# An iterated layer-norm stage: where the constant is added, how two of eight tiles are centred, and how the bias products are shaped

## The reference, cut to what matters

```
def _L1_ffn_ref(x, ln_w, ln_b, W, b):        # C = 128, EPS = 1e-5, 30 iterations
    def step(h, _):
        h = h + 0.01 * jnp.tanh(h)
        h = h * jax.nn.sigmoid(h)
        h = _layernorm(h, ln_w, ln_b)
        h = jnp.einsum('bsc,dc->bsd', h, W) + b
        return (h, None)
    x, _ = jax.lax.scan(step, x, None, length=N_ITERS)
    return x
...
x = x + _L1_ffn_ref(_layernorm(x, axis=-1), ...)
```

## Time and profile before

| | us |
|---|---|
| median of 3 runs | 1390.7 (1389.99 to 1391.48) |
| the profiled execution | 1390.53 |
| its span, first to last instruction | 1388.6 |
| TensorE's share of the chain of waits that ended last | 78% |
| granted TensorE clock, mean over the span | 0.985 of full speed |
| the iterated stage in it, from about 616 to 1364 | 748 |

### The profile page before, as it was taken

One profiled execution on the slowest core, in us unless ns is written; L12 is line 12 of the kernel. 1 busy time (PEld: TensorE's weight loads), 2 busy tenths in 40 slices (PEclk: granted clock), 3 DMA queues, 4 the chain that ended last, 5 costly groups with the idle time before them and its releaser, 6 DMA issues.

```text
span 1388.6 us, 28231 instructions
## 1 busy us (share of the span) xinstructions
PE 1332.4 (96%) x8786; PEld 1085.0 (78%) x8786; DVE 1234.2 (89%) x2774; ACT 1011.1 (73%) x1373; POOL 948.3 (68%) x749
## 2 busy tenths in 40 slices
PE   4899999999999999869999999999999999999998
PEld 3677777777777776558888888888888888888887
DVE  6678888887788886599999999999999999999997
ACT  1344444444444444569999999999999999999994
POOL 2244444444444444269999999999999999999995
PEclk9899999999999999969999999999999999999999
DMA  5111111111111100000000000000000000000004
GB/s 178 39 39 38 38 38 38 38 38 38 38 38 38 37 0 1 0 1 0 0 0 0 0 0 0 0 0 0 0 0 0 0 0 0 0 0 0 0 0 122
DMA packets 29790, 27.68 MB, mean 20 GB/s; under 512 B 3269, under 2 KB 21448, under 8 KB 29640
## 3 DMA queue, kind: packets, MB, share of 16 engines
q1 hardware_dynamic: 29768, 27.41, 6.2%
HBM read 23.21 MB, written 4.19 MB: 20 GB/s over the span
## 4 chain that ended last, share of the span: by engine, by line
PE 78%; DVE 11%; issue 4%; ACT 3%; POOL 1%; SPq 1%; DMA 0%; DVEq 0%; ACTq 0%; POOLq 0%
PE psum L751 34%; PE psum L763 15%; PE psum L747 6%; PE psum L553 4%; PE psum L555 4%; PE psum L554 4%; PE psum L694 3%; PE psum L570 2%; PE psum L575 2%; ACT emb_f L855 2%; PE psum L584 2%; DVE emb_n L1177 1%; DVE x_less_n L1161 1%; PE psum L564 1%; DVE xh L1059 1%
## 5 line engine op out<-in xcount | busy, mean ns | idle before, releaser
L751 PE MATMUL psum<-w_t,y_all 128*128 128x128 f32 x3840 | 493.7, 282 | 0.0
L751 PEld LDWEIGHTS psum<-w_t,y_all 128*128 128x128 f32 x3840 | 447.9, 192 | 54.5 <-issue 54.5
L454 POOL TENSOR_TENSOR f_rs<-f_var,half_neg 128x8 f32<-128x8 f32 x240 | 410.4, 1710 | 49.2 <-DVE f_var L1116 30.2
L1091 DVE BATCH_NORM_STATS2 f_stat<-g_ring 128x6 f32<-128x256 f32 x960 | 340.7, 413 | 3.9 <-ACT g_ring L813 3.9
L458 POOL TENSOR_TENSOR h_ring<-g_ring,f_rs 128x640 f32<-128x640 f32 x240 | 302.5, 1260 | 18.8
L1107 DVE SCALAR_TENSOR_TENSOR u_ring<-t_ring,psum 128x1024 f32<-128x1024 f32 x232 | 278.1, 1199 | 0.0
L763 PE MATMUL psum<-ident,h_ring 128*128 128x128 f32 x1920 | 250.6, 274 | 6.4 <-DVE h_ring L1080 6.4
L813 ACT ACTIVATE g_ring<-u_ring 128x1024 f32<-128x1024 f32 x240 | 253.5, 1056 | 0.8 <-DVE u_ring L1107 0.8
L836 ACT ACTIVATE y_all<-psum 128x1024 f32<-128x1024 f32 x240 | 243.7, 1015 | 8.4 <-PE psum L763 8.4
L822 ACT ACTIVATE t_ring<-psum 128x1024 f32<-128x1024 f32 x232 | 238.6, 1029 | 13.5 <-PE psum L751 4.9
L763 PEld LDWEIGHTS psum<-ident,h_ring 128*128 128x128 f32 x1920 | 219.1, 142 | 7.1 <-issue 3.8
(11 more groups left out here) (158 smaller groups left out, 1774.3 us busy)
## 6 DMA issues: line engine op xcount, KB each, us to landing
work<-in_adj_dram SPq DMA_DIRECT2D x16, 1024.0 KB, 5.4
x_tok<-in_x_dram SPq DMA_DIRECT2D x16, 256.0 KB, 5.5
out_dram<-y_all SPq DMA_DIRECT2D x8, 512.0 KB, 3.3
work<-in_L_gnn_conv_w_dram SPq DMA_DIRECT2D x1, 1088.0 KB
work<-in_L_gnn_w_ih_dram SPq DMA_DIRECT2D x1, 384.0 KB
work<-in_L_gnn_w_hh_dram SPq DMA_DIRECT2D x1, 192.0 KB
work<-in_L_gnn_W_dram SPq DMA_DIRECT2D x1, 64.0 KB, 5.1
work<-in_L_ffn_weight_dram SPq DMA_DIRECT2D x1, 64.0 KB, 4.8
```

Source lines behind the costliest of these rows:

```text
L454: pool.tensor_tensor(f_rs[:, j % 4, :], f_var[:, j % 2, :], half_neg[:, 0:GT], ALU.pow).then_inc(f_pow, 1)
L751: m = pe.matmul(y_ps[k % 2][:, h, C * t:C * t + C], y_all[:, GT * k + NT * h + t, :], w1_t[:], start=False, stop=True, skip_group_check=True)
L1091: ins = dve.bn_stats(f_stat[:, j % 2, q, :], both)
```

## The change

It has four parts.

1. **The constant.** `f_stat` gets a second plane that is filled with C * EPS once. `f_var` is now the sum over the pair (sum of squares, constant), a `tensor_reduce` of 8 x 2 values in place of the `tensor_scalar`.
2. **VectorE's two tiles are centred.** They are now tiles 6 and 7 of the group (they were 5 and 6), ScalarE's is tile 5. VectorE's `tensor_scalar` subtracts the mean, read from `f_stat`, and multiplies by `f_rs`: two per-partition scalars in place of one. `f_stat` has four buffers in place of two, and `bn_stats` waits for the normalisation that read the old one.
3. **These tiles bring their bias.** Their last channel isn't transposed (127 of 128 columns): row 127 of these places in `g_ps` holds ones, set once ahead of the stage (`s_ones`), and the copy to `y_all` takes them along. Their product is with `w1c_t`, from whose rows the last channel's was subtracted, and whose last row is the bias.
4. **Bias products of 768 columns.** Six tiles still need the bias product. The three parts stand on rows 0, 32 and 64 of a `bias1` of 65 rows; the product for the first bank has 512 columns, that for the second 256, and the second stands after the first bank's products.

Preparation grows: one more transpose and one more ScalarE copy (`w1c_t`), the making of its source in `fold`, twelve copies of one row in `split_bias` for seven operations on all rows that went, a fill of `f_stat` and `bias1`, and two fills of 32 x 256 in PSUM.

```
-        f_stat = sb("f_stat", [P, 2, GT // 2, 6])
+        f_stat = sb("f_stat", [P, 4, 2, GT, 3])
...
                     for h in range(2):
-                        rows = slice(HALF * h, HALF * h + HALF)
-                        pe.matmul(y_ps[k % 2][:, h, :], ones_bf[rows, :], bias1[rows, :, :].rearrange("p t c -> p (t c)"),
+                        biased = min(NT, centred - NT * h)
+                        pe.matmul(y_ps[k % 2][:, h, 0:C * biased], ones_bf[:],
+                                  bias1[:, 0:biased, :].rearrange("p t c -> p (t c)"),
                                   start=True, stop=False, skip_group_check=True)
-                    for h in range(2):
                         for t in range(NT):
-                            m = pe.matmul(y_ps[k % 2][:, h, C * t:C * t + C], y_all[:, GT * k + NT * h + t, :], w1_t[:],
-                                          start=False, stop=True, skip_group_check=True)
+                            m = pe.matmul(y_ps[k % 2][:, h, C * t:C * t + C], y_all[:, GT * k + NT * h + t, :],
+                                          w1_t[:] if t < biased else w1c_t[:], start=False, stop=True, skip_group_check=True)
...
                     for t in range(GT):
-                        m = pe.transpose(g_ps[j % 2][:, t // NT, P * (t % NT):P * (t % NT) + P],
-                                         tiles(h_ring[j % 4])[:, t, :], ident[:])
+
+                        rows = P if t < GT - DVE_TILES[j] else P - 1
+                        m = pe.transpose(g_ps[j % 2][0:rows, t // NT, P * (t % NT):P * (t % NT) + P],
+                                         tiles(h_ring[j % 4])[:, t, 0:rows], ident[:])
...
+                dve.wait_ge(s_wturn0, 1)
+                link(dve.tensor_scalar(nat[:, N_W0, :], w1_nat, w1_nat[:, C - 1:C], None, ALU.subtract))
+                dve.tensor_copy(nat[:, N_W0, C - 1:C], vec(FB1))
+                for r in range(3):
+                    dve.tensor_copy(b1_cols[:, 32 * r:32 * r + 1], vec(FB1))
...
                 for t in range(NT):
-                    dve.scalar_tensor_tensor(out=bias1[:, t, :], in0=part_bf[:, 2, :], scalar=row_of[:, 2:3],
-                                             in1=part_f[:, 1, :], op0=ALU.mult, op1=ALU.add)
+                    for r in range(3):
+                        dve.tensor_copy(bias1[32 * r:32 * r + 1, t, :], part_bf[32 * r:32 * r + 1, r, :])
...
-                    first = GT - ACT_TILES[j] - DVE_TILES[j]
-                    for t in range(first, first + DVE_TILES[j]):
+                    for t in range(GT - DVE_TILES[j], GT):
                         ins = dve.tensor_scalar(tiles(h_ring[j % 4])[:, t, :], tiles(g_ring[j])[:, t, :],
-                                                f_rs[:, j % 4, t:t + 1], None, ALU.mult)
+                                                f_stat[:, j % 4, 0, t, 1:2], f_rs[:, j % 4, t:t + 1],
+                                                ALU.subtract, ALU.mult)
                     ins.then_inc(f_norm_dve, 1)
...
                     dve.wait_ge(f_silu, s + 1)
-                    wait(dve, f_v, s - 1)
+                    wait(dve, f_v, s - 3)
+                    wait(dve, f_norm_dve, s - 3)
...
-                    squares = f_stat[:, j % 2, :, :].rearrange("p q (o w) -> p (q o) w", w=3)[:, :, 2]
-                    dve.tensor_scalar(f_var[:, j % 2, :], squares, C * EPS, None, ALU.add).then_inc(f_v, 1)
+                    squares = f_stat[:, j % 4, :, :, 2].rearrange("p o t -> p t o")
+                    dve.tensor_reduce(f_var[:, j % 2, :], squares, AX_X, ALU.add).then_inc(f_v, 1)
```

58 lines of the change are left out of this document (32 added, 26 removed).

## The result

| | before | after |
|---|---|---|
| device time, median (range) | 1391.09 us (1389.99 to 1391.65) | 1356.68 us (1355.54 to 1357.76) |
| span of the profiled execution | 1388.6 us | 1355.7 us |
| first and last steady `f_var` | 618.8, 1362.9 | 622.1, 1331.1 |
| pace of the steady slots | 3.221 us | 3.069 us |
| mean granted clock of TensorE | 0.985 | 0.981 |

The pace is the mean distance between the starts of two steady `f_var`, and so the length of one slot. The ratio of the times is 0.9753, with a 95% interval of 0.9737 to 0.977: 34 us faster. The forecast was 1359.

The account below looks back on a forecast made before the run. A 3.24 us loop through VectorE's `f_var` and GpSimd's power and five tiles bounds most slots. Pace 3.22 to 3.08 saves 32.5 us over 232 slots, preparation adds 1: span 1357.1, time 1359 us, range 1352 to 1387.

Parts of the forecast that it names:

- Pace: Steady slots of the stage: 3.08 us a slot instead of 3.22, saving 32.5 us over 232 slots.
- four close loops: Own loops per slot: ScalarE 3.06, VectorE 3.06, GpSimd 3.01, TensorE 3.00 us; tied by waits, they add 0.02.
- The constant: VectorE's `f_var` as a reduction isn't held while GpSimd works and costs 0.08 us a slot instead of 0.38.
- Centred tiles: VectorE's two tiles: the second scalar adds 0.12 us a slot; being held by GpSimd's tiles costs nothing.
- the loop through the power: VectorE's `f_var`, GpSimd's power and five tiles, then the next `f_var`, held until they end: 3.24 us before the change.
- TensorE: Its own loop per slot falls from 3.18 to 3.00 us with 65-row bias products; bounds 3.00 to 3.61.
- the switches: Two switches around TensorE's 64-row bias products, together 0.31 us of its 3.18 us slot, expected to go.
- Preparation: Ahead of the stage: copies, a transpose and PSUM fills add about 1 us, from 0 to 3.
- End: The eight slots of the last iteration already run without most of the waits, so nothing is saved there.
- A (partial switching): Part of TensorE's switching stays, or latencies bite: pace 3.12 to 3.20, 1368 to 1387 us; chance 0.15.
- B (held): VectorE's reduction is held like the old `f_var`, the 3.24 us loop stays: 1391.7 us; chance 0.10.
- C: TensorE becomes the bound through bfloat16 bias and float32 product changes: 1482 or 1433 us; chance 0.13 with other losses.

Follow-up runs that it names:

- the kernel without both edits: The changed kernel without ScalarE's tile (GpSimd's last tile is transposed twice instead) and without the mean's subtraction in VectorE's two tiles: 1347.88 us.
- first experiment: The kernel before with only the constant changed, `f_var` becoming a reduction over the pair; old tiles, 64-row bias pair and weights stay: 1381.48 us, ratio 0.9932.

## Why the prediction was right, point by point

*Pace.* Forecast 3.08, measured 3.069. The bound was named as ScalarE's and VectorE's 3.06, tied, and the kernel without both edits shows the tie. The 0.02 that I added for four close loops was 0.01: 2.5 us of the 35.1 saved in the steady slots.

*The constant.* Forecast 0.08 and not held; measured 0.08 start to start, 164 ns long. The first experiment shows it by itself. The Trainium skill's "SBUF — State Buffer", section "SBUF: two separate sides", has the lock between VectorE and GpSimd, and "VectorE: DVE Perf Modes" the one mode of `tensor_reduce`. The traces agree with the lock where the five tiles are concerned: the old `f_var` and a tile that meets them from the start last until they end, the reduction doesn't. They don't agree with a lock for a whole instruction where the power is concerned: in the changed kernel the second tile mostly starts less than 0.05 us behind a power of 1.64 us, and lasts 0.33 to 0.37, as the first tile does ahead of it. The mode of an instruction is in no trace. The second page's advice to restructure a reduction on a hot path would have cost 20 us here (1376.6 against 1356.7).

*Centred tiles.* Forecast +0.12 a slot, measured +0.11 (0.51 instead of 0.40), and a short hold in 13 of 231 steady slots, at no cost, as forecast. What I missed is that the tiles move the power's length by 0.08 us. Both lengths stood in the rows, 1.72 and 1.64, and I took the first for granted in the stage. It cost nothing in the forecast, since the loop through the power was no longer the longest, but it made the expectation for the kernel without the reduction wrong by 15 to 20 us.

*TensorE.* Forecast 3.00 with the switches gone, measured 3.05 with a little waiting in it (the transposes to the next bias take 0.93, where eight are 0.88; without the wait it is 3.00). The pair put back gives 3.180, the forecast's 3.18.

*Preparation.* Forecast +1, from 0 to +3; the profiled executions show +3.3. This term was mis-sized for them, and wrongly made up: the twelve copies, the fills and the transposes that I counted can't be seen in the time, while 1 us comes from graphs that take 0.07 us longer each, which I hadn't thought of, and some 2 from where the half-clock stretch of TensorE falls. Another pair of executions would give another number: the kernel before profiled again starts its steady slots at 616.8 us, 2 earlier, and the changed kernel again at 623.7, 1.6 later. The median times differ by 34.4 us; with the other two pieces as they are, 35.1 and 1.1, that leaves +1.8. That the total came out 2 us from the forecast is in part luck, since a pace that was better than forecast covers this term.

*End.* Forecast nothing for the last slots, since they run without most of the waits; measured -1.1 us. The reason given is what failed here: where nothing holds TensorE, as in the earlier trace rows, its own slot counts, and that is the one that got shorter. The nine profiles without the 64-row pair take 24.4 to 24.7 us from the last steady `f_var` to the end, the five with it 25.7 to 26.9. It offsets a third of the miss before it.

*Rivals.* A (partial switching) is out by the 0.22 from the bias to the products behind it and the 9.4 us of issue idling. B (held) is out by 205 ns at most. C would have needed TensorE's slot over 3.22. As for the sum, this is saved by part: the reduction alone 9.5 us of steady slots, the rest alone (3.222 - 3.154) x 231 = 15.6, both 35.1. They are worth 10 us more together, since each uncovers what the other removes.

## What to carry to other kernels

Where several engines run in step, write down each one's own loop and every loop that passes through two of them, then rank them: a change is worth the distance to the next on the list, and two changes together can be worth more than their sum. A null result of one experiment doesn't clear an engine that ties with another; take from both at once. A tiny instruction on the path between two engines can cost as much as a large one, and a form with more work in it (a reduction of twice the values, a second scalar) can be the cheaper one if it isn't held.

## What I had not expected of the hardware

- ScalarE's recorded durations stretch when it has no slack: the same tanh is 1029 ns long on average in the kernel before, 1420 and 1763 in two executions of the changed kernel, 1798 without the mean's subtraction, 1024 where ScalarE idles 0.18 us a slot. The distance from its start to the next one's is 0.90 to 0.92 us in all of them.
- GpSimd's power of eight values per partition is 1.64 us long, but 1.72 or 1.73 when a one-scalar tile of VectorE has begun 0.04 to 0.07 us ahead of it, and 1.85 in 13 cases beside a two-scalar tile. So the two engines hold each other in both directions, and 0.06 us in the spacing of VectorE's tiles (0.20 or 0.26 apart) is worth 0.07 us a slot where the loop through the power is the longest.
- TensorE's granted clock near 50 us, in nearly the same code, came out at 0.50 in one kernel's execution and 1.00 in another's; the way from the first graph to the second is 35.3 us with 3 us at half clock and up to 38.5 with 10.
